# Output biases of a mixture-of-experts layer: from TensorE's products to gathered rows and VectorE

## What is computed

```python
gates = softmax(xf @ gate_w + gate_b)                    # 2048 tokens, 16 experts
topv, topi = top_k(gates, 2)
combine = sum(one_hot(topi) * topv[..., None], axis=1)
h  = gelu(einsum('nd,edh->neh', xf, ew1) + eb1)
eo = einsum('neh,ehd->ned', h, ew2) + eb2                # eb2: 16 x 512
routed = einsum('ned,ne->nd', eo, combine)
hs = gelu(einsum('nd,sdh->snh', xf, sw1) + sb1)          # 2 shared experts, 2048 hidden each
shared = einsum('snh,shd->nd', hs, sw2) + sum(sb2, axis=0)
x + shared + routed                                      # xf is layernorm(x)
```

## Time and profile before

| | us |
|---|---|
| median of 3 runs | 869.34 |
| the profiled execution | 869.32 |
| its span, first to last instruction | 867.7 |
| around the span | 1.6 |
| PE busy | 842.0 (97%) |
| DVE busy | 598.4 (69%) |
| ACT busy | 471.7 (54%) |
| POOL busy | 192.4 (22%) |
| TensorE's granted clock | 1.000 |

### The profile page before, as it was taken

The page is one execution under the profiler, slowest core; times in us unless marked ns, Lnnn a source line. Parts: engine busy times, 40 slices in busy tenths (PEclk is TensorE's granted clock), DMA queues, the critical chain, the costliest instruction groups (busy, mean ns, idle before and its releaser), DMA issues.

```text
span 867.7 us, 14418 instructions
## 1 busy us (share of the span) xinstructions
PE 842.0 (97%) x4134; PEld 699.5 (81%) x4134; DVE 598.4 (69%) x1280; ACT 471.7 (54%) x843; POOL 192.4 (22%) x229
## 2 busy tenths in 40 slices
PE   3799999999999999999999999999999999999998
PEld 2567888888888888888888888888888889998886
DVE  8887898976677778556787786555687544443684
ACT  4687876454476554445556464345456356556441
POOL 4101000012100000112000002111121488754880
PEclk9999999999999999999999999999999999999999
DMA  8903644377352332584433324555697388868976
GB/s 217 291 30 97 159 133 134 98 153 145 83 164 89 100 107 85 115 199 86 146 111 98 96 86 96 122 101 169 178 230 179 104 255 283 262 212 272 321 220 217
DMA packets 127405, 135.45 MB, mean 156 GB/s; under 512 B 10520, under 2 KB 88912, under 8 KB 126828
## 3 DMA queue, kind: packets, MB, share of 16 engines
q1 hardware_dynamic: 117612, 108.47, 46.5%
q0 software_dynamic: 8784, 25.11, 9.7%
q10 hardware_dynamic: 944, 1.07, 0.4%
HBM read 111.63 MB, written 22.98 MB: 155 GB/s over the span
## 4 chain that ended last, share of the span: by engine, by line
PE 93%; ACT 0%; issue 0%; DVE 0%; ACTq 0%
PE up L638 13%; PE up L640 13%; PE up L639 13%; PE acc L704 13%; PE acc L701 13%; PE acc L699 13%; PE up L890 5%; PE acc L638 1%; PE acc L639 1%; PE acc L640 1%; PE misc L664 1%; PE up L664 1%; PE acc L815 1%; PE misc L723 1%; PE up L807 1%; PE misc L731 0%
## 5 line engine op out<-in xcount | busy, mean ns | idle before, releaser
L638 PE MATMUL up<-xs,w1hi 128*128 128x512 f32 (+1 forms) x512 | 199.0, 389 | 0.0
L640 PE MATMUL up<-xs,w1lo 128*128 128x512 f32 (+1 forms) x512 | 196.2, 383 | 0.0
L639 PE MATMUL up<-xs,w1hi 128*128 128x512 f32 (+1 forms) x512 | 195.7, 382 | 0.0
L699 PE MATMUL acc<-w2hi,hhi 128*128 128x512 f32 x486 | 189.9, 391 | 0.0
L701 PE MATMUL acc<-w2lo,hhi 128*128 128x512 f32 x486 | 189.6, 390 | 0.0
L968 ACT ACTIVATE hhi<-up,b_col 128x512 fp32r<-128x512 f32 x128 | 86.4, 675 | 155.0 <-PE up L640 130.6
L1253 DVE TENSOR_TENSOR hlo<-hf,hhi 128x512 fp32r<-128x512 f32 x128 | 85.7, 669 | 71.9 <-ACT hf L971 30.3
L704 PE MATMUL acc<-w2hi,hlo 128*128 128x512 f32 x486 | 131.0, 390 | 0.0
L638 PEld LDWEIGHTS up<-xs,w1hi 128*128 128x128 f32 x512 | 96.3, 188 | 18.8 <-issue 0.5
L640 PEld LDWEIGHTS up<-xs,w1lo 128*128 128x128 f32 x512 | 96.3, 188 | 18.9
L639 PEld LDWEIGHTS up<-xs,w1hi 128*128 128x128 f32 x512 | 96.5, 188 | 18.2
(11 more groups left out here) (283 smaller groups left out, 1081.1 us busy)
## 6 DMA issues: line engine op xcount, KB each, us to landing
w_raw<-in_L_ffn_sw SPq DMA_DIRECT2D x256, 256.0 KB, 3.1
expert_rows<-ysb SPq DMA_DIRECT2D x47, 256.0 KB, 3.4
xn_rows<-kn POOLq DMA_DIRECT2D x16, 256.0 KB, 7.5
e2raw<-in_L_ffn_ew SPq DMA_DIRECT2D x16, 256.0 KB, 5.1
ew_sb<-in_L_ffn_ew SPq DMA_DIRECT2D x16, 256.0 KB, 6.8
X<-in_x SPq DMA_DIRECT2D x12, 256.0 KB, 7.5
vin<-in_ctx SPq DMA_DIRECT2D x12, 256.0 KB, 11.2
out<-X SPq DMA_DIRECT2D x12, 256.0 KB, 5.1
```

The costliest lines, as they stand in the source:

```text
L638: nc.tensor.matmul(o, lhs[0], rhs[0], start=start, stop=False)
L639: nc.tensor.matmul(o, lhs[0], rhs[1], start=False, stop=False)
L640: return nc.tensor.matmul(o, lhs[1], rhs[0], start=False, stop=stop)
L699: nc.tensor.matmul(acc[t][:], hh, w2hi[:, slot], start=first and (q > 0 or t >= HT) or again, stop=False)
```

## The change

- PE: the bias products are gone (L717 three times four, L937 four times), and so is the transposition of cb96 (L745, 16 times). The rank products now wait for "mem" of the tile's routing steps and not for "lo". The stop flag sits on the last down product.
- DVE: route_combine and the product for comb2 are gone. route_pick also writes the chosen experts' numbers to bias_at (int32). A new route_bias(q, t - 1), at j = 1 behind x_lo, does for the tile before: X2 row tile += gate 0 x gathered row 0, += gate 1 x gathered row 1, += bias_s, three dependent instructions on 128 x 512. The last tile's stands at late(2) of block 3. take_block waits for the last down product and for the biases of all the block's tiles but the last, whose bias is added in the next block's first tile.
- POOL: at j = 1 gather_bias(t) waits for route_bias(t - 1), copies the tile's two columns of numbers, and issues two indirect DMAs that read eb2 from HBM into bias_g, 256 KB each, before the tile's scatter.
- ACT: combine_T and the three roundings of the bias table are gone.
- SP: the six bias loads ahead of the first weights and their wait are gone; behind the first nine chunks' loads it waits for the zeroed slot table (bias_s takes the room of zero_i) and loads the two rows of sb2, broadcast, 256 KB each. The store of rows_kept moves from the start of block q to behind the loop, and there ahead of load_quad(q + 2), since the last tile's bias comes only in block q.

The diff, cut to its core:

```diff
             def routing_products(t):
-                pe.wait_ge(rt.sem, rt.at(t, "lo"))
-                nc.tensor.transpose(misc[0:BR, CBT0:CBT0 + P], cb96[:], ident[:])
+                pe.wait_ge(rt.sem, rt.at(t, "mem"))
                 nc.tensor.matmul(misc[:, RANK0:RANK0 + E], tri[:], member[:], start=True, stop=False)
...
-                        pe.wait_ge(cbt_ok, TB * (q + 1))
-                        for t in range(TB):
-                            last = nc.tensor.matmul(acc[t][:], cbT[:, t], bias_r[:], start=False, stop=True)
-                        last.then_inc(acc_ready, 1)
...
+            def route_bias(q, t):
+                rows = X2[:].rearrange("p q t d -> p (q t) d")[:, t]
+                gate = c_all[:].rearrange("p n j -> p (n j)")
+                dve.wait_ge(bias_in, 32 * (t + 1))
+                need(dve, acc_free, TB * q)
+                for j in range(2):
+                    if j:
+                        dve.wait_ge(bias_ok, 3 * t + 1)
+                    V.scalar_tensor_tensor(out=rows, in0=bias_g[:, j], scalar=gate[:, bass.ds(2 * t + j, 1)], in1=rows,
+                                           op0=ALU.mult, op1=ALU.add).then_inc(bias_ok, 1)
+                after(con, 0, "shb")
+                dve.wait_ge(bias_ok, 3 * t + 2)
+                V.tensor_tensor(rows, rows, bias_s[:], ALU.add).then_inc(bias_ok, 1)
...
             def take_block(q):
 
-                dve.wait_ge(acc_ready, q + 1)
+                dve.wait_ge(down_done, CH * (q + 1))
+                dve.wait_ge(bias_ok, 3 * (TB * (q + 1) - 1))
...
                     if j == 1:
-                        route_combine(t)
                         if q < NQ - 1:
                             if q:
                                 dve.wait_ge(up_done, CH * q)
                             x_lo(tb, q % 2, t + TB, misc)
+                        if not isinstance(t, int) or t:
+                            route_bias(q, t - 1)
...
+            def gather_bias(t):
+                pool.wait_ge(rt.sem, rt.at(t, "bi"))
+                if isinstance(t, int) and t == 0:
+                    pool.wait_ge(con.sem, con.at(0, "shb"))
+                else:
+                    pool.wait_ge(bias_ok, 3 * t)
+                at = bias_at[:].rearrange("p n j -> p (n j)")
+                G.tensor_copy(bias_stage[:], at[:, bass.ds(2 * t, 2)]).then_inc(bst, 1)
+                pool.wait_ge(bst, t + 1)
+                apart(pool)
+                for j in range(2):
+                    pool.indirect_dma_start(out=bias_g[:, j], out_offset=None, in_=eb2[:, :],
+                                            in_offset=bass.IndirectOffsetOnAxis(ap=bias_stage[:, j:j + 1], axis=0))\
+                        .then_inc(bias_in, 16)
...
-                if q in (1, 2):
-                    sp.wait_ge(acc_free, TB * q)
-                    sp.dma_start(keep_dram[q - 1], X2[:, q - 1].rearrange("p t d -> p (t d)")).then_inc(keep_out, 16)
...
+                if q in (1, 2):
+                    sp.wait_ge(acc_free, TB * q)
+                    sp.wait_ge(bias_ok, 3 * TB * q)
+                    sp.dma_start(keep_dram[q - 1], X2[:, q - 1].rearrange("p t d -> p (t d)")).then_inc(keep_out, 16)
                 if q + 2 < NQ:
                     load_quad(q + 2)
```

More of the change, by code:

```diff
@@ L355, in mixed_layer @@
         gsm = Steps(sem("gsm"), "parts high lg max sub sum rec gates")
[L356 to L357 removed]
+        rt = Steps(sem("rt"), "gt max idx idxf c e bi o1 o2 mem rank m1 m2 pos pint pall msum")
+        con = Steps(sem("con"), "keep0 keep1 first0 boost0 cap shift c0 c1 half ms ones o16 gz qz pz ghi glo shb")
         pcon = Steps(sem("pcon"), "ramp id0 tri0 id tri ie eb thr ip tok stage z")
@@ L702, in __new__ @@
                     need(pe, h_lo, c + 1)
+                    ends = isinstance(c, int) and n == CH - 1
                     for t in tiles:
@@ L705, in __new__ @@
                                                 start=False,
-                                                stop=isinstance(c, int) and c == HOLD - 1 and acc[t] in y_bank)
+                                                stop=ends or isinstance(c, int) and c == HOLD - 1
+                                                and acc[t] in y_bank)
                     last.then_inc(down_done, 1)
@@ L935, in _ @@
                     nc.tensor.matmul(acc[t][:], hhi[:, slot, tok], w2lo[:, slot], start=False, stop=False)
-                    nc.tensor.matmul(acc[t][:], hlo[:, slot, tok], w2hi[:, slot], start=False, stop=False)
-                nc.tensor.matmul(acc[t][:], cbT[:, t], bias_r[:], start=False, stop=True).then_inc(tile_ready, 1)
+                    last = nc.tensor.matmul(acc[t][:], hlo[:, slot, tok], w2hi[:, slot], start=False,
+                                            stop=c == NCH - 1)
+                last.then_inc(tile_ready, 1)
         @block.scalar
@@ L1062, in split_e2 @@
                 nc.scalar.copy(e2hi[:, e], e2raw[:, e]).then_inc(r2hi, 1)
-            def combine_T(t, tb, q):
-                act.wait_ge(rank_ps, t + 1)
-                need(act, acc_ready, q)
-                nc.scalar.copy(cbT[:, tb], misc[0:BR, CBT0:CBT0 + P]).then_inc(cbt_ok, 1)
             nc.scalar.preload_act_table_set("natural_log_exp_and_others")
@@ L1136, in _ @@
             table_relu(11)
-            act.wait_ge(c_in, 16 * 10)
-            for at in (0, 32, 64):
-                nc.scalar.copy(bias_r[at:at + 32], bias_f[at:at + 32]).then_inc(bias_hi, 1)
             for n in range(11, 13):
@@ L1641, in _ @@
             const(V.memset(ones16[:], 1.0))
-            const(V.memset(cb96[:], 0.0))
-            after(con, 0, "cb0")
-            const(V.memset(cb96[:, E:E + S_EXP], 1.0))
-            const(V.memset(cb96[:, 32 + E:32 + E + S_EXP], 1.0))
             const(V.memset(f(gw2[:]), 0.0))
@@ L1768, in late @@
                         slots()
+                    if j == 2:
+                        route_bias(NQ - 1, NT - 1)
                 def cdo(ins):
```

79 lines of the change are left out of this document (28 added, 51 removed).

## The result

The changed kernel takes 863.75 us (median of four runs, 863.26 to 863.79) beside 869.36 us for the kernel before (869.12 to 870.53): a ratio of 0.9932, with a 95% interval of 0.992 to 0.9944. The prediction was 863.8 us in a range of 862.6 to 866.8. So far it was right. The kernel before stayed within 868.8 and 871.3 us in all its 63 runs. So the change also brought a spread. The prediction's thin cover is one cause of it that the runs show; how much of it that explains stays open.

The account below looks back on a forecast made before the run. PE was taken to bound the kernel from about 69 us to the end. Bias products 3.7 plus transposition 1.8 make 5.5 us, other terms 0: 869.3 less 5.5 gives 863.8 us, range 862.6 to 866.8.

Parts of the forecast that it names:

- thin cover: At block 1's end, the w2 load comes 3.6 to 6.3 us later against a margin of 6.05 us.
- narrower forecast: Whole kernel: the time lies at 863.2 to 864.6 us; chance 0.55.
- Bias products, 3.7 us: On PE, 16 bias products at 0.2325 us each leave the saturated stretch: 3.7 us less.
- Transposition, 0.11 us each: On PE before the rank products, 16 transpositions of cb96 go at 0.11 us each: 1.8 us less.
- gives nothing: Rival on PE: removing the transposition gains nothing, only 3.7 us go: 865.6 us; chance 0.10.
- gives more: Rival: the transposition gives nearer its recorded 273 ns, or the start gets shorter: 861.2 us; chance 0.05.
- ACT, the start: ACT's dropped copies and roundings take no time off; the start changes by 0, within 0.3 us either way.
- DVE's additions: On DVE, three dependent instructions add 2.2 us a tile, 35 us in all, and stall PE by 0.
- Gathers: On POOL, two indirect DMAs a tile: issue 2.9 us, landing 7 us (ends 4.9 and 7.7), PE stall 0.
- if gathers land after 10 us: Sign in the profile after: gathers landing after 10 us would show the prediction wrong.
- The moved store: At block 1's end, 1 MB of store and 0.5 MB of gather delay the w2 load 3.6 to 6.3 us; stall 0.
- backlog reaches PE: Rival at block 1's end: the late loads make PE wait, 1 to 3 us once, 864.8 to 866.8; chance 0.16.

Follow-up runs that it names:

- the run that was caught: The changed kernel itself, unaltered, measured again in eight runs (median 865.08 us); the profile fell on the run of 867.36 us.
- the kernel with both places mended: Changed kernel with store behind the block's last chunk loads, tail order 2, 0, 1, 3, last group of additions behind last low part: 863.84 us.

## Why the prediction was right, point by point

The range held both medians, 863.75 and 865.08 us; the narrower forecast, 863.2 to 864.6, held the first and missed the second.

- **Bias products, 3.7 us**: right, 3.8 measured (0.23 to 0.24 at the blocks' ends, 0.25 at the kernel's end).
- **Transposition, 0.11 us each**: mis-sized. The distance to the next start is not all that it costs; the products behind it start later too. Taken away it gives 0.15 and put back it takes 0.13, and 0.03 more come with the rest of what went. The tile shrank by 0.18 us: 2.9 us in place of 1.8. Whether the 0.03 are ACT's copy or DVE's small instructions stays open. The rival "gives nothing" fell; "gives more" was half right.
- **ACT, the start**: 0, right; PE's block 0 gate products start 0.15 us earlier.
- **DVE's additions**: 1.53 and 0.69 us as predicted. Block 0, tile 1: w2lo ends at 192.3 us and the products with w2lo begin at 194.57, so 2.3 us are left (1.9 predicted). Block 3, tile 14: low part done at 644.6, read at 648.10, 3.5 us (3.7 predicted). DVE's waits for ranks are gone in blocks 1 and 2. PE doesn't wait between 69 and 690 us, and DVE's busy time rose by 19.9 us (20 predicted).
- **Gathers**: the landing was 4.8 us, not 7; the issue took 3.8 us from the copy's start to the second DMA's end, not 2.9, because of a 0.81 us wait between POOL's copy and its first DMA that no earlier row had. The two errors cancel in part. The 4.8 is a median: one gather of block 0 (second issue at 194.04) took 10.2 us, which by the prediction's own sign, "if gathers land after 10 us", was a warning; it cost DVE a wait and PE none. DVE waited 0.43 us in block 3, and 1.18 us once in block 0, for that gather, where I had expected nothing. By the Trainium skill, "SBUF — State Buffer", section "SBUF: two separate sides", an issue could be held by a two-input DVE instruction; the bias gathers show little of it (1.12 us on average), the tail much, as the last section shows.
- **The moved store**: the step that failed, though its sum held. The predicted delay of 3.6 to 6.3 us "against 6.05" was 3.3 us for w2 in the first profile, by the margin that it left, and then the w1 load behind it was the thinner one (2.0 us left). ACT's wait for w2 was 5.05, 5.79, 6.79, 7.00, 7.10 and 7.83 us in the six traces with the store moved once, and 1.89 to 3.08 us in the six with the store elsewhere (the kernel with three gathers in a row left out): 4 us more by the store, and 3 us of difference between executions of about the same program. I had taken one value and asked whether it fits. So the rival "backlog reaches PE" is no alternative to the forecast: it happens in part of the executions of one kernel. Its price, "1 to 3 us, once", was too low: 4.0 us in the run that was caught, half of it wait, half of it clock. The 0.5 MB of a gather, which I had put into that sum with the Trainium skill's "DMA: Bandwidth & Descriptors", section "Issuing engines are not separate DMA queues", can't be found there: without gathers ACT waited 7.00 us, and 7.10 in the kernel before with only the store moved.
- **The tail**: not in the prediction at all. In the traces the stretch from the last routed product to the first of the last tiles took 71.5 to 73.9 us, 71.56 in the kernel before and 72.96 and 72.52 in the changed one. Where it was longest, PE waited for low parts that stood behind the last gathered rows. Whether that is a price of the change is open: the kernel before, the one without bias products and the one with only the store moved have 71.53 to 71.56, and each of the other eleven traces has more, 71.58 to 73.92. Neither the gathers of the biases nor the store are needed for it (73.92 without the gathers; 72.28 in the kernel before without products and transposition, where the store stands in its old place). Also, "every start follows the one before" up to the last product was not quite so even in the kernel before, where PE stood for 0.43 us at 702.31 and 0.27 us at 786.03.
- **The sum**: products 3.8, transposition and what went with it 2.9, the start 0.15, less 1.4 in the tail, 5.5 us, and the last product starts 5.5 us earlier: the total as predicted, from four terms of which the second was mis-sized by 1.1 us and the last was not foreseen at all, and these two nearly cancel. That was luck in part: a second profile of the same kernel has a span 2.0 us shorter than before, and not 5.5.

## What to carry to other kernels

What leaves the engine that is always busy leaves the time, and what comes to others is free as long as every wait is shorter than its cover, in the worst execution and not in the profiled one: ask of every cover how much the waiting time varies, and run the kernel often enough to see it. A store that is moved ahead of loads in a full stretch delayed them here by about its size over the stretch's rate; if nobody waits for the store, issue it behind them. And before work is moved behind the critical engine's last need, look for what is stored after it.

## What the hardware did that was not expected

A wait of PE of 1.91 us was followed by some 3.4 us at 1.2 GHz, in which the products started 0.43 us apart. In the kernel with the store three times the clock fell while PE still waited (granted clock 0.97 from 386 to 387 us, 0.50 from 387 to 388), and the products behind the wait of 5.17 us ran at the lower level until between 393 and 394. The bill beyond the wait was 2.0 and 2.5 us. The waits of 0.3 to 1.64 us in the tails were not followed by it. And longer waits aren't always: in the kernel whose second gather waits for the first, two waits of PE in block 3, and then windows over them (PE, PEld, DVE, ACT, POOL busy, granted clock, DMA share, GB/s):

```profile
645.44 0.47 PE L696 MATMUL acc<-w2hi,hhi 128*128 128x512 f32 x1 [3.92 <-issue]
661.36 0.47 PE L696 MATMUL acc<-w2hi,hhi 128*128 128x512 f32 x1 [3.04 <-issue]
```

```profile
646.00:650.00 4.00, 4.00 (x12) 3.12 (x11) 3.62 (x21) 0.00 (x0) 0.17 (x1) 0.57 0.93 235
658.00:668.00 10.00, 6.96 (x31) 5.53 (x30) 9.41 (x22) 3.63 (x7) 4.06 (x3) 1.00 0.44 122
```

The wait of 3.92 us was followed by a lower clock, the one of 3.04 us and the 2.55 us at 238.20 (granted clock 1.00 from 235 to 245) were not. So a wait of 2 to 3 us may be paid once or with some 2 us on top, and its length alone didn't decide which.

POOL's issues of indirect DMAs can take 4.63 us where they take 0.95. POOL and DVE in the tail of the changed kernel:

```profile
802.14 1.14 POOL L2050 DMA_INDIRECT yg<-expert_rows,row_all  x1 [0.30 <-issue]
803.59 4.63 POOL L2050 DMA_INDIRECT yg<-expert_rows,row_all  x1 [0.30 <-issue]
808.52 1.02 POOL L2050 DMA_INDIRECT yg<-expert_rows,row_all  x1 [0.31 <-issue]
```

```profile
801.05 2.74 DVE L1859 SCALAR_TENSOR_TENSOR X<-yg,c_all,X 128x512 f32<-128x512 f32 x4 [2.54 <-DMA yg<-expert_rows,row_all]
803.70 0.68 DVE L1231 TENSOR_TENSOR hlo<-hf,hhi 128x512 fp32r<-128x512 f32 x1
...
806.72 0.68 DVE L1243 TENSOR_TENSOR w1lo<-w_raw,w1hi 128x512 fp32r<-128x512 f32 x1
807.32 2.73 DVE L1859 SCALAR_TENSOR_TENSOR X<-yg,c_all,X 128x512 f32<-128x512 f32 x4
```

DVE's scaled additions of expert rows are the four of L1859. The long issue begins with a run of six low parts and ends 0.8 us after it; the issues beside the four scaled additions (from 801.05 on) take their usual time. A run of three low parts makes 2.83 us of an issue, one of six 4.63. The 32 issues of the tail took 51.2 to 58.4 us in the traces, by how they fell. In the two traces with the most, 58.1 and 58.4 us, PE lost the most in the tail; but the kernel with both places mended had 57.9 us and a tail of 71.92, and between 51 and 57 us there is no order. So that the long issues are what makes the rows late for PE is argued and not shown. The Trainium skill, "SBUF — State Buffer", section "SBUF: two separate sides", describes a lock on a shared port pair that is held for a whole instruction. If that is what holds the issue, which no run here tests, it is held here for a whole run of instructions. That the scaled additions, which have two SBUF inputs as well, don't hold an issue, is not what the section says.
